# One product for key and query angles, new instruction lists, banks and waits, and expert counts from sums of two blocks

## What is computed

```python
h = concat(tokens(x), txt)                       # (128, 325, 128)
n = layernorm(h)
key = exp(1j * pi * tanh(n @ Wk + bk))           # 32 angles a token
qry = exp(1j * pi * tanh(n @ Wq + bq))           # 32 angles a token
# for each set of 8 angles: causal sum of key * V, read with conj(qry), weighted by softmax(set_weights)
total = gate * sets + (1 - gate) * sigmoid(pos_weight) * positions
h = h + n + total / sqrt(8 * position) @ Wo + bo
n2 = layernorm(h)
e1, e2 = top_2(sigmoid(n2 @ gate_w.T))           # 64 experts, capacity 256, in token order
h = h + shared(n2) + sum_r weight_r * expert_r(n2)
```

## Time and profile before

| what | us |
|---|---|
| median of 3 runs | 1766.22 |
| lowest and highest | 1763.71, 1768.30 |
| the profiled execution, its own time | 1764.47 |
| its span, first to last instruction | 1762.70 |
| TensorE busy in the span | 1569.5 (89%) |
| VectorE busy | 1511.0 (86%) |
| ScalarE busy | 1101.5 (62%) |
| GpSimd busy | 1226.0 (70%) |
| mean granted TensorE clock | 0.958 of full speed |

### The profile page before, as it was taken

How to read it: one execution, slowest core, us unless ns; L and a number is a source line. 1 busy time by engine, 2 the same in 40 slices (tenths; PEclk the granted TensorE clock), 3 DMA queues, 4 the chain that set the end, 5 groups by cost and what they waited for, 6 DMA issues and landing times. The chain is left out here.

```text
span 1762.7 us, 34557 instructions
## 1 busy us (share of the span) xinstructions
PE 1569.5 (89%) x9606; PEld 1162.9 (66%) x9606; DVE 1511.0 (86%) x6004; ACT 1101.5 (62%) x1869; POOL 1226.0 (70%) x1162
## 2 busy tenths in 40 slices
PE   2799999999999999999999999999999982676662
PEld 1577777777777777777777777777777761455551
DVE  2589999999999999999999999999999983687761
ACT  2877777777777777777777777777777631111110
POOL 0117777777777777777777777777777777588888
PEclk9899999999999999999999999999999995798885
DMA  9866766666666666666666666666666201576653
GB/s 172 226 160 141 136 135 130 128 122 126 118 115 114 112 111 111 108 108 108 108 108 110 109 107 107 107 109 108 110 108 106 57 17 34 96 114 99 98 79 33
DMA packets 259956, 194.19 MB, mean 110 GB/s; under 512 B 65513, under 2 KB 239268, under 8 KB 259656
## 3 DMA queue, kind: packets, MB, share of 16 engines
q1 hardware_dynamic: 206008, 173.72, 52.3%
q0 software_dynamic: 51200, 17.87, 8.5%
q10 hardware_dynamic: 2576, 0.60, 0.4%
HBM read 84.84 MB, written 83.73 MB: 96 GB/s over the span
## 5 line engine op out<-in xcount | busy, mean ns | idle before, releaser
L556 POOL DMA_INDIRECT slot_rows<-xs,slot x768 | 823.6, 1072 | 219.5 <-issue 219.5
L549 POOL TENSOR_TENSOR rs<-ve,neg_half 128x6 f32<-128x6 f32 x128 | 172.0, 1343 | 245.8 <-DVE ve L1219 245.8
L615 ACT ACTIVATE img<-img 84x980 f32<-84x980 f32 (+1 forms) x192 | 341.7, 1781 | 0.5 <-DMA img<-img 0.4
L832 PE MATMUL bank<-img,w_tok 126*128 126x392 f32 (+1 forms) x640 | 224.0, 497 | 10.9 <-DMA img<-img 10.9
L596 POOL DMA_INDIRECT out_rows<-img,etok x128 | 199.5, 1559 | 29.7 <-issue 29.7
L832 PEld LDWEIGHTS bank<-img,w_tok 126*128 126x128 f32 (+1 forms) x640 | 117.9, 192 | 83.9 <-issue 13.4
L668 ACT ACTIVATE xs<-h,nb,rs 128x128 f32<-128x128 f32 x384 | 154.7, 481 | 28.5 <-DVE nb L1279 28.5
L913 PE MATMUL bank<-a_t,v 128*128 128x325 f32 (+2 forms) x768 | 167.0, 353 | 1.4 <-DVE a_t L1273 1.4
L895 PE MATMUL bank<-pos_a,v 128*128 128x325 f32 (+2 forms) x768 | 167.6, 353 | 0.0
L684 ACT ACTIVATE xh<-h,nb,rs 128x128 f32<-128x128 f32 x384 | 154.0, 482 | 3.6 <-DVE nb L1279 3.6
L913 PEld LDWEIGHTS bank<-a_t,v 128*128 128x128 f32 (+1 forms) x768 | 130.1, 190 | 28.2 <-issue 1.9
(11 more groups left out here) (192 smaller groups left out, 3669.8 us busy)
## 6 DMA issues: line engine op xcount, KB each, us to landing
img<-in_x SPq DMA_DIRECT2D x384, 150.1 KB
img<-img SPq DMA_DIRECT2D x256, 160.8 KB
img<-img SPq DMA_DIRECT2D x128, 128.6 KB
out_rows<-fin SPq DMA_DIRECT2D x128, 128.0 KB
slot_rows<-xs,slot POOLq DMA_INDIRECT x768
slot_rows<-init_rows SPq DMA_DIRECT2D x16, 540.0 KB, 5.4
img<-slot_rows SPq DMA_DIRECT2D x32, 270.0 KB, 3.3
h<-in_txt SPq DMA_DIRECT2D x64, 128.0 KB, 2.7
```

Of the source, the lines that this page charges most:

```text
L549: g.tensor_tensor(out=rs[:, q.u], in0=ve[:, q.u], in1=neg_half[:, :], op=ALU.pow).then_inc(s_rs, 1)
L556: g.indirect_dma_start(out=slots_d, out_offset=bass.IndirectOffsetOnAxis(ap=slot[0:nt, q.x, r, part:part + 1], axis=0), in_=xs[0:nt, q.x, ...
L615: a.activation(cols[:, b0:b0 + nb, :], raw[:, q.u, :].rearrange("p (t b) -> p b t", b=P)[:, b0:b0 + nb, :], ACT.Copy)\
L832: ins = mm(bank[:, 4, 0:2 * PATCHES], w_tok[r, m, :], xk[r, k.u, :, m, :], start=(m == 0), stop=(m == SHIFT - 1))
```

## The change

The kernel keeps its two stages, its tiling and all its outputs. In the first stage:

1. Key and query angles come from one product for each sample, with the 128 columns key, key, query, query (`wkq[:, 0]`), and for the second sample query, query, key, key (`wkq[:, 1]`): `angles_1` and `angles_0` instead of `queries` and `keys`. The query waves then stand on the other 64 partitions than the key waves; `moved_queries`, new on ScalarE, copies them over and multiplies them by the set weight. `scaled_query` on VectorE is gone, and the factor by position moves into the mask (`maskn` instead of `mask`, `wn` and `invn` dropped).
2. The expert counts: the absent rows of the 69-token tiles get an expert index beyond 63 (a constant `absent`, added in `indices`, which was a copy), so that all blocks can be summed over 128 rows. `block_pairs`, new on VectorE, adds blocks two by two. `counts` is then 5 products instead of 7: the triangle, one that adds the first block of each two to the second, and three for the sums of two.
3. The lists of all five engines are in a new order, with four pairs behind (`p4`) on VectorE and three on TensorE. The angles, `values`, `shared_3a` and `shared_3b` move to the next step.
4. Nearly every product has another bank, and many waits are dropped or changed, where the order of the lists makes them needless.
5. In SP's list the loads of images are issued four pairs ahead instead of three, behind the six other transfers; the reordering of the second pair's image moves from ahead of the wait for `s_setup` to behind it.

```diff
-            def scaled_query(y):
-                dve.wait_ge(S["a_sin"], y.count())
-                wait(dve, S["pe_sc"], y, 2)
-                TT(qn[:, y.u, :], kq[:, y.u, 1, :], wn[:, :], ALU.mult).then_inc(S["v_qn"], 1)
...
+            def moved_queries(k):
+                act.wait_ge(S["a_sin"], k.count())
+                for s in range(2):
+                    to, at = slice(64 * s, 64 * s + 64), slice(64 - 64 * s, 128 - 64 * s)
+                    ins = a.activation(qs[to, k.u, :], kq[at, k.u, s, :], ACT.Identity, scale=wcol[at, 4:5])
+                ins.then_inc(S["a_qs"], 1)
...
-            def keys(k):
-                wait(pe, S["v_su"], k, 2)
-                for s in range(2):
-                    ins = mm(bank[64 * s:64 * s + 64, 6, 0:L], wk[:, :], x_t[:, s, :], start=True, stop=True)
-                ins.then_inc(S["pe_k"], 1)
-            def queries(k):
-                pe.wait_ge(S["a_xt"], k.count())
-                wait(pe, S["v_su"], k, 2)
-                for s in range(2):
-                    ins = mm(bank[64 * s:64 * s + 64, 7, 0:L], wq[:, :], x_t[:, s, :], start=True, stop=True)
-                ins.then_inc(S["pe_q"], 1)
+            def angles_1(k):
+                pe.wait_ge(S["a_xt"], k.count())
+                mm(bank[:, 3, 0:L], wkq[:, 1, :], x_t[:, 1, :], start=True, stop=True).then_inc(S["pe_k1"], 1)
+            def angles_0(k):
+                mm(bank[:, 2, 0:L], wkq[:, 0, :], x_t[:, 0, :], start=True, stop=True).then_inc(S["pe_k0"], 1)
...
+            def block_pairs(w):
+                dve.wait_ge(S["v_both"], w.count())
+                pairs = both[:, 0:2 * NT, :].rearrange("p (j i) e -> p j i e", i=2)
+                TT(two[:, :, :], pairs[:, :, 0, :], pairs[:, :, 1, :], ALU.add).then_inc(S["v_bp"], 1)
...
             def counts(w):
-                pe.wait_ge(S["v_both"], w.count())
-                wait(pe, S["a_g"], w, -2)
+                pe.wait_ge(S["v_bp"], w.count())
                 flat = both[:, :, :].rearrange("p t e -> p (t e)")
                 n = 2 * NT + 1
-                mm(bank[:, 3, 0:n * E], below[:, :], flat, start=True, stop=False)
-                for i in range(2 * NT):
-                    nt = TILES[i % NT][1]
-                    src = both[0:nt, i:i + 1, :].to_broadcast([nt, n - 1 - i, E])
-                    ins = mm(bank[:, 3, (i + 1) * E:n * E], ones[0:nt, :], src, start=False, stop=(i == 2 * NT - 1))
+                mm(bank[:, 5, 0:n * E], below[:, :], flat, start=True, stop=False)
+                halves = bank[:, 5, 0:2 * NT * E].rearrange("p (j i e) -> p j i e", i=2, e=E)
+                mm(halves[:, :, 1, :], ones[:, :], both[:, 0:2 * NT, :].rearrange("p (j i) e -> p j i e", i=2)[:, :, 0, :],
+                   start=False, stop=False)
+                for j in range(NT):
+                    c = 2 * j + 2
+                    ins = mm(bank[:, 5, c * E:n * E], ones[:, :], two[:, j:j + 1, :].to_broadcast([128, n - c, E]),
+                             start=False, stop=(j == NT - 1))
                 ins.then_inc(S["pe_pf"], 1)
```

More of the change, by code:

```diff
@@ L119, in runs, with uses, steps, wait @@
     def runs(self):
[L120 removed]
+        return 0 <= self.c < PAIRS
     def count(self):
[L124 to L151 removed]
+        return self.c + 1
+    def uses(self, of):
+        return self.c // of + 1
+def first(pair):
+    return pair.c == 0
+def steps(body, begin, end):
+    for k in range(begin, PAIRS + end):
+        body(Pair(k))
+def wait(eng, sem, pair, back):
     q = pair.back(back)
[L154 removed]
+    if q.runs():
         eng.wait_ge(sem, q.count())
@@ L1050, in body @@
-                if y.runs():
-                    project(y)
-                if k.runs():
-                    queries(k)
-                    keys(k)
-                    values(k)
-            steps(pe, body)
+                if p1.runs():
+                    project(p1)
+                if p2.runs():
+                    logit_rows(p2)
+            steps(body, 0, 3)
             def turn(q):
@@ L1442, in body @@
             def body(k):
[L1443 removed]
+                p1 = k.back(1)
+                p2 = k.back(2)
+                p3 = k.back(3)
+                p4 = k.back(4)
+                if p1.runs():
+                    image_stats(p1)
+                if p4.runs():
+                    score(p4)
+                if p3.runs():
+                    bias_scale_2(p3)
+                if p1.runs():
+                    moments_1(p1)
+                if p4.runs():
+                    indices(p4)
@@ L1520, in prepare @@
+                if p3.runs():
+                    score_low(p3)
+                if p2.runs():
+                    scaled_2(p2)
+                if p3.runs():
+                    shared_product(p3)
+                    top_indices(p3)
+                if p1.runs():
+                    value_rows(p1)
+            steps(body, 0, 4)
             def prepare(q):
```

716 lines of the change are left out of this document (337 added, 379 removed).

## The result

| | before | after |
|---|---|---|
| median (us) | 1765.73 (4 runs) | 1717.67 (4 runs, 1715.9 to 1718.0) |
| ratio | | 0.9725, 95% interval 0.9708 to 0.9742 |
| span of the profiled execution | 1762.70 | 1714.0 |
| mean granted TensorE clock | 0.958 | 0.958 |

The direction was right, the size was not.

The account below looks back on a forecast made before the run. The prediction took TensorE as full, with VectorE nearly in balance. Its terms summed to -0.48 us a step, times 62 is -29.8, with +1 for the ends -29: 1737 us from 1766.2, range 1720 to 1757 for 8 in 10.

Parts of the forecast that it names:

- Angles: TensorE's angle products merged to full width: -0.14 us a step, bounds 0 and -0.25; `moved_queries` on ScalarE hidden.
- Counts: TensorE's `counts` in 5 products instead of 7: -0.22 us a step; the product behind it pays +0.08.
- Waits and order: TensorE's small losses at `gates` (-0.05), `position_out` (-0.08) and `phase_out` (-0.07) a step should go; dropped waits cost nothing.
- GpSimd and transfers: GpSimd's list stays 19.1 us a step with gaps; its new waits and the image loads are hidden.
- Start and drain: Ends of the first stage: +3 us at the start, -2 in the drain, together +1, between -4 and +6.
- B: Rival: VectorE takes over as the bound, a step is 21.5 us, time 1751; chance 0.15.
- C: Rival: GpSimd's list becomes the bound, a step is 22.2 us, time 1794; chance 0.05.
- E: Rival: no change, TensorE's saved restarts and waits come back elsewhere, within 5 us of 1766; chance 0.06.
- D: Rival: GpSimd's `rstd_2` holds VectorE's `top_indices` by the port lock, a step is 21.93 us, time 1777; chance 0.04.

Follow-up runs that it names:

- b_all_3: Kernel before, in its old order, banks and waits, with full-width angle products, no `scaled_query`, new counts with `block_pairs`, no `moved_queries`: 1763.03 us beside 1765.72.
- a_both_undone: Changed kernel with both the old 64-column angle halves and the old seven counts products put back: 1752.86 us, ratio to before 0.9926.
- a_halves: Changed kernel with each angle product made as two halves of 64 columns, as before: 1736.75 us, 19.1 us more than the changed kernel.
- a_oldcounts: Changed kernel with the old seven products in counts, `block_pairs` still run but unused: 1731.23 us, 13.6 us more than the changed kernel.
- a_dve1: Changed kernel with one more VectorE product of 128 x 325 per step, read by nobody, ahead of `token_sum`: 1716.99 us.
- a_dve3: Changed kernel with three more VectorE products of 128 x 325 per step, ahead of `token_sum`: 1720.54 us.
- a_swap: Changed kernel with `logits` ahead of `shared_1a` on TensorE, so two boundaries between product forms instead of three: 1712.52 us.

## Why the prediction was wrong

The two orders and the two sets of products, each measured (the usual step in us, and the median time):

| | old products | new products |
|---|---|---|
| old order | 21.76, 1765.7 | 21.74, 1763.0 (`b_all_3`) |
| new order | 21.61, 1752.9 (`a_both_undone`) | 21.01, 1717.7 |

*Angles: mis-sized, and the main failure.* The prediction gave -0.14, with -0.25 as a bound "if `values` behind them also loses its restart". `a_halves` measured 0.34. The products themselves give the -0.14 as worked out; `values` gives 0.10 and `project`, ahead of them, another 0.10, so the truth lay beyond the bound. The price stood in the kernel before: `shared_1a`, which the earlier trace rows and the rows above put at 0.64, stands ahead of the 64-column `logits`, and a product between two of its own form takes 0.55. Only a 0.55 was read there.

*Counts: -0.22 forecast, -0.27 in the rows, 0.25 by `a_oldcounts`.* The restart of the product behind them, +0.08, came as forecast (0.72 for `shared_1a`, against 0.64).

*Waits and order: the three stalls.* Forecast -0.20; `gates` -0.06, `position_out` -0.05, `phase_out` -0.08, and `scores` -0.03: -0.22. With the old products the new order gives 0.15. That fits the rows: -0.22 of stalls and +0.08 for the product behind `counts`. The sizes were right, the account was incomplete. The prediction said that TensorE "is ahead by a little", which the rows bear out, and then added its savings as if nothing else stood close behind. But by the rows two loops through VectorE's list stood there, at 21.70 and 21.63. `b_all_3`, with less work on TensorE in the old order, gave 2.7 us. In the new lists `image_rows` stands ahead of `gate`, `image_stats` follows `value_rows` directly, and `token` writes a bank that does not wait for `second_rows`; by the lists and waits, these open both loops. So nearly all of the gain on the products hangs on the part that the forecast priced at 0.20.

*GpSimd and transfers.* Nothing was late, as forecast, but the margin is thin: GpSimd's waits for data are 7.9 + 6.8 = 14.7 us in 22 steps, 0.7 a step, where the earlier trace rows has 2.66. Its list occupies 21.0 - 0.7 = 20.3 us and not 19.1, since its busy time grew from 15.7 to 16.5 a step. Most of that is the scatter instruction, 1132 ns instead of 1072 on average, 12 a step; no run tells why.

*Start and drain.* Forecast +3 and -2, together +1; the start cost 1.3, the drain gave 3.35, and with the 0.3 behind it the sum is -1.8. No run tested it.

The gap in all: (0.756 - 0.48) x 62 = 17.1 us of the steps and 2.8 of the ends make 19.9, and the spans differ by 48.7 where 28.8 were forecast. Of the 0.276 a step the angles are 0.20, the counts 0.05 and the stalls 0.02.

*Rivals.* B (VectorE as the bound, 1751) is false: `a_dve1` costs nothing, `a_dve3` 3 us. VectorE's busy time fell to 442.01 / 460 x 21.01 = 20.2 a step, less than the 20.5 forecast, though `scaled_query`, which the sum took off with its duration of 0.50, is only 0.40 from start to start. C (GpSimd) did not come, though it was nearer than its chance said. E did not come: of the restarts only the one priced at +0.08 appeared elsewhere. D, the port lock, did not come. The timelines of GpSimd and of VectorE in the changed kernel:

```profile
714.73 1.38 POOL L544 TENSOR_TENSOR rs<-ve,neg_half 128x6 f32<-128x6 f32 x1
```

```profile
715.19 0.22 DVE L1419 FIND_INDEX8 topi<-top,lg 128x8 uint32<-128x64 f32 x1
```

`top_indices` did fall beside `rstd_2` (714.73 to 716.11), and a search takes 0.22 inside it (715.19) and behind it (716.16). But it was no test of the rule, and the prediction misread it: a search is a MATCH_VALUE_LOAD, which reads the 8 values to look for, and then a FIND_INDEX8, for which the trace lists one source, 128 x 64. The kernel before has a test. Its addition `ms` of two SBUF operands (L1202) lies wholly inside the `pow` 61 times and takes 0.17 there, as it does the 3 times that it lies outside. The Trainium skill (SBUF — State Buffer, section "Who interferes with whom") says that a VectorE instruction with two SBUF inputs contends with a GpSimd instruction that reads SBUF; this trace shows no such hold.

*Open.* That less work on TensorE alone would have taken at most 0.06 a step off the kernel before is worked out from its rows, and `b_all_3` agrees; but that kernel also changes VectorE's list, and no edit of TensorE's products alone has shown it, since those sent for it ran where the kernel before took 2078 us or more. Also, which of the new places (bank, `image_stats`, `image_rows` ahead of `gate`) opens the loop was read from the traces and not tried one by one.

## What to carry to other kernels

A product of another form costs its neighbours on both sides; look in the trace for any product beside such a change and compare it with one between its own kind, and put forms of one kind together (`a_swap`). An engine that looks 99 or 100% busy may be held by a loop through another engine's list: take the end of one instruction, follow the waits round to the same instruction a step later, and see whether the length is the step. If it is, or is within a few hundredths of it, cutting the busy engine's work gives next to nothing until the order opens the loop.

## What the runs showed of the hardware

- A change between 128- and 64-column products cost 0.09 to 0.10 us on each side, in three places (around `logits` and around the angle products before, and in `a_halves`), and the weight load behind it started with its product instead of 0.1 us or more ahead.
- In the changed kernel VectorE took one more instruction of 128 x 325 while it looked 96% busy (442.01 of 460 us), and the step did not change; with three it was busy for 99% (456.68) and the step grew by 0.05 us.
- `moved_queries`, two ScalarE instructions that read 64 partitions and write the other 64, took 1.14 us together, against 0.53 for one of 128 x 325 (the tanh of an angle product, same trace).
- In the kernel before, VectorE additions of two SBUF operands (L1202) took 0.17 us inside a GpSimd `pow` that reads SBUF, 61 times, and 0.17 us outside it, 3 times.
